# A layer of differential attention: FFN at other steps, a coefficient on GpSimd, and both maps' exponentials in SBUF

## The reference

```
q1,q2,k1,k2,v = xn @ Wqkv.T + b      # 16 q heads, 8 k heads of 128, 4 v heads of 256
p = softmax(q1 k1 / sqrt(128)) - lam * softmax(q2 k2 / sqrt(128))     # causal
o = rmsnorm(p @ v) * subln_w * (1 - lambda_init);  s = o @ out_w.T + out_b
g = silu(quant4(xn) @ quant4(Wffn).T + bias)   # blocks of 32 rounded to a 4-bit float
x = x + s * g
```

## Time and profile before

| | us |
|---|---|
| runs | 1752.3, 1755.01, 1758.83 |
| median | 1755.01 |
| the profiled execution's own time | 1754.4 |
| its span | 1752.6 |

### The profile page before, as it was taken

How to read it: one execution, slowest core, us unless ns; L and a number is a source line. 1 busy time by engine, 2 the same in 40 slices (tenths; PEclk the granted TensorE clock), 3 DMA queues, 4 the chain that set the end, 5 groups by cost and what they waited for, 6 DMA issues and landing times. The chain is left out here.

```text
span 1752.6 us, 28521 instructions
## 1 busy us (share of the span) xinstructions
PE 1538.7 (88%) x9137; PEld 899.8 (51%) x9153; DVE 1196.0 (68%) x3177; ACT 885.8 (51%) x2542; POOL 662.4 (38%) x1161
## 2 busy tenths in 40 slices
PE   2666588999989988999889988999989989899898
PEld 1343355555555555545555555545555546555554
DVE  4467777776777677776677667775777767675682
ACT  4563356535663456535664356634564356533561
POOL 2103542345324443344424443244424443243433
PEclk7778799999999999999999999999999999999999
DMA  7401334333342334333352334324342333422433
GB/s 250 140 4 27 64 67 82 61 88 70 50 91 55 84 73 82 64 78 72 55 87 57 84 73 79 68 46 100 55 85 54 95 63 65 80 54 67 64 76 73
DMA packets 385353, 130.63 MB, mean 75 GB/s; under 512 B 366354, under 2 KB 366900, under 8 KB 385204
## 3 DMA queue, kind: packets, MB, share of 16 engines
q1 hardware_dynamic: 385204, 128.81, 35.4%
HBM read 31.74 MB, written 8.39 MB: 23 GB/s over the span
## 5 line engine op out<-in xcount | busy, mean ns | idle before, releaser
L690 ACT ACTIVATE ph<-ps,small 128x128 f16<-128x128 f32 (+3 forms) x256 | 134.4, 525 | 395.0 <-DVE ps L981 394.4
L1168 POOL TENSOR_SCALAR norm<-psum_l,small 128x1 f32<-128x1 f32 x256 | 88.4, 345 | 584.9 <-ACT pp L681 584.9
L970 DVE CUSTOM_DVE_ANT_0 ps<-ps,mask,ssc 128x384 f32<-128x384 f32 (+3 forms) x512 | 279.7, 551 | 35.9 <-PE ps L547 35.4
L490 PE MATMUL ps<-xT,wqkv 128*128 128x512 f16 x768 | 297.6, 387 | 6.8 <-DVE qkv L940 6.4
L491 PE MATMUL ps<-xT,wqkv 128*128 128x512 f16 x768 | 296.4, 386 | 0.0
L492 PE MATMUL ps<-xT,wqkv 128*128 128x512 f16 x768 | 295.5, 385 | 0.0
L940 DVE SCALAR_TENSOR_TENSOR qkv<-ps,bsc,qkv 128x512 f16<-128x512 f32 x192 | 143.3, 750 | 187.0 <-ACT qkv L658 187.0
L490 PE MATMUL ps<-qkv,pT 128*128 128x256 f16 x640 | 179.6, 281 | 74.3 <-DMA pT<-ph 73.5
L545 PE MATMUL ps<-qkv 128*128 128x384 f16 (+3 forms) x512 | 155.2, 309 | 56.5 <-DVE ph L987 53.6
L490 PE MATMUL ps<-wout,heads 128*128 128x512 f16 x512 | 194.1, 379 | 0.5 <-DVE small L956 0.5
L491 PE MATMUL ps<-wout,heads 128*128 128x512 f16 x512 | 194.0, 379 | 0.0
(11 more groups left out here) (147 smaller groups left out, 3146.9 us busy)
## 6 DMA issues: line engine op xcount, KB each, us to landing
xin<-in_L_attn_hidden_states SPq DMA_DIRECT2D x8, 1024.0 KB, 5.8
xres<-in_L_attn_hidden_states SPq DMA_DIRECT2D x32, 256.0 KB, 2.8
out_x<-res SPq DMA_DIRECT2D x32, 256.0 KB, 2.4
qkv<-in_L_attn_Wqkv_w SPq DMA_DIRECT2D x8, 512.0 KB, 7.3
heads<-in_L_attn_Wqkv_w SPq DMA_DIRECT2D x8, 512.0 KB, 10.7
pT<-ph SPq DMA_TRANSPOSE x256, 2.7
heads<-on SPq DMA_TRANSPOSE x256, 2.5
qkv<-in_L_attn_out_w SPq DMA_DIRECT2D x4, 512.0 KB, 5.6
```

The costliest lines, as they stand in the source:

```text
L490: mm(out, ah, bh, start=start and j == 0, stop=False)
L690: run(ph[:, n % PH, 0:w], sc_ps[u][:, 1, 0:w], ACT.Copy, scale=sigma).then_inc(ph_hi, 1)
L970: nc.vector.tensor_tensor_reduce(sc, sc, mask[:, S - w:S], ssc[:, c:c + 1], BIG, ALU.add, ALU.min, ebias[:, u, m:m + 1]).then_inc(max_done, 1)
```

## The change

Six things are changed together.

- The ffn fills move from steps 10 to 13 to steps 22 to 25, and group 2's v fills from 15 and 16 to 14 and 15. In steps 24 and 25 the ffn fill is ahead of the next batch's k fill in the list. The transposes of `aq` move one step later, to 10 and 11.
- Reciprocal and coefficient are computed by GpSimd in `eps_of`, by a pow with exponent -1 and a tensor_scalar, ahead of the instruction that stood there alone.
- `pp` holds both maps. Map 0 is now first in `maxima` and `exps`. Both exponentials go to `pp`, combine reads and writes `pp`, and `p_hi` and `p_lo` read it.
- `scores(n)` waits for the exponentials of step n - 2.
- `xh` lies in `gate`, with a wait of the ffn fill's first write for the transpose of `x`; the first and second split move one step earlier. In the last batch the first load of `xres` waits for the second ffn fill.
- `square_o` writes its unused squares to PSUM, and the identity of the setup lies in `pT`.

```
-PH = 4 - AHEAD
+PH = 2
-FFN_STEP = 10
+FFN_STEP = 22
-        at = (None, PROJ_AT, PROJ_AT[:6] + (7, 8), (0, 1, 1, 2, 3, 3, 4, 5))[g]
+        at = (None, PROJ_AT, PROJ_AT, (0, 1, 1, 2, 3, 3, 4, 5))[g]
-X_SPLIT = {15: 0, 17: 1, 18: 2, 19: 3}
+X_SPLIT = {14: 0, 16: 1, 18: 2, 19: 3}
-        pp = sb("pp", [P, S], F32)
+        pp = sb("pp", [P, 2, S], F32)
-        xh = [t[:].bitcast(F16).rearrange("p (s h) -> p s h", s=2) for t in (res, xres)]
-        xh += [aq[:, 2 * u:2 * u + 2, :].bitcast(F16) for u in range(2)]
+        xh = [gate[:, k, :].bitcast(F16).rearrange("p (s h) -> p s h", s=2) for k in range(NT)]
+        junk = [ps[:, 6, E:2 * E], ps[:, 7, E:2 * E]]
...
-                if b == B - 1 and s == LAST_STEP:
+                if b == B - 1 and s == FFN_STEP + 3:
+                    sp.wait_ge(fill_done, fill_of("ffn", b, 0, 1) + 1)
                     residual(b, 0)
-                for k in {FFN_STEP - 1: (0, 1), FFN_STEP: (2, 3)}.get(s, ()):
+                for k in {10: (0, 1), 11: (2, 3)}.get(s, ()):
...
-                wait(pe, ph_lo, n - 1)
+                wait(pe, exp_done, 2 * n - 2)
...
-                for a, m in enumerate((1, 0)):
+                for a, m in enumerate((0, 1)):
                     act.wait_ge(max_done, 2 * n + a + 1)
                     sc = sc_ps[u][:, m, 0:w]
-                    if m == 0:
-                        wait(act, comb_done, n)
-                    run(sc if m else pp[:, 0:w], sc, ACT.Exp, bias=ebias[:, u, m:m + 1], scale=-1.0,
+                    wait(act, ph_lo if m else comb_done, n)
+                    run(pp[:, m, 0:w], sc, ACT.Exp, bias=ebias[:, u, m:m + 1], scale=-1.0,
...
-                run(ph[:, n % PH, 0:w], sc_ps[u][:, 1, 0:w], ACT.Copy, scale=sigma).then_inc(ph_hi, 1)
+                run(ph[:, n % PH, 0:w], pp[:, 1, 0:w], ACT.Copy, scale=sigma).then_inc(ph_hi, 1)
...
                     wait(dve, gated, f.gate - NT + 1)
+                    if f.gate // NT + 1 < B:
+                        dve.wait_ge(xT_done[j], 16 * (f.gate // NT + 2))
...
-                dve.wait_ge(exp_done, 2 * n + 2)
-                nc.vector.reciprocal(recip[:], l2).then_inc(recip_done, 1)
-                dve.wait_ge(recip_done, n + 1)
-                ts(coef[:, u:u + 1], l1, recip[:], neglam, ALU.mult, ALU.mult).then_inc(coef_done, 1)
                 dve.wait_ge(coef_done, n + 1)
-                stt(out=sc_ps[u][:, 1, 0:w], in0=sc_ps[u][:, 1, 0:w], scalar=coef[:, u:u + 1], in1=pp[:, 0:w],
+                stt(out=pp[:, 1, 0:w], in0=pp[:, 1, 0:w], scalar=coef[:, u:u + 1], in1=pp[:, 0, 0:w],
...
-                stt(out=ph[:, n % PH, w:2 * w], in0=sc_ps[u][:, 1, 0:w], scalar=sigma, in1=ph[:, n % PH, 0:w],
+                stt(out=ph[:, n % PH, w:2 * w], in0=pp[:, 1, 0:w], scalar=sigma, in1=ph[:, n % PH, 0:w],
...
                 pool.wait_ge(exp_done, 2 * n + 2)
+                pt(recip[:], l2, minusone, ALU.pow).then_inc(recip_done, 1)
+                pool.wait_ge(recip_done, n + 1)
+                nc.gpsimd.tensor_scalar(coef[:, n % 2:n % 2 + 1], recip[:], l1, neglam, ALU.mult, ALU.mult)\
+                  .then_inc(coef_done, 1)
                 wait(pool, on_lo, n - 5)
                 nc.gpsimd.tensor_scalar(nr[:, 0:1], l1, l1, eg[:, g:g + 1], ALU.mult, ALU.mult).then_inc(eps_done, 1)
```

More of the change, by code:

```diff
@@ L207, in build @@
         on = sb("on", [P, 2, 2, 2, P], F16)
-        junk = sb("junk", [P, E], BF16)
         v32 = sb("v32", [P, 2, E], F32)
@@ L211, in build @@
         xres = sb("xres", [P, HID], F32)
-        ident = sb("ident", [P, P], F32)
         mask = sb("mask", [P, S], BF16)
@@ L218, in build @@
         bnat = v32[0:34, 0, 0:P]
-        lam4, lam2 = pp, v32[:, 1, :]
+        lam4, lam2 = pp[:, 0, :], v32[:, 1, :]
         t2 = v32[:].rearrange("p a e -> p (a e)")
@@ L222, in build @@
                for t in (xres, res) for u in range(2)]
-        xh = [t[:].bitcast(F16).rearrange("p (s h) -> p s h", s=2) for t in (res, xres)]
-        xh += [aq[:, 2 * u:2 * u + 2, :].bitcast(F16) for u in range(2)]
+        xh = [gate[:, k, :].bitcast(F16).rearrange("p (s h) -> p s h", s=2) for k in range(NT)]
         spare = pT[:, 1, :, :].rearrange("p c t -> p (c t)").bitcast(F32)
         bT = spare[:, 0:34]
+        ident = spare[:, 256:384]
         babs, bgrp, bound = [spare[:, 64 + 32 * t:96 + 32 * t].rearrange("p (g c) -> p g c", g=G) for t in range(3)]
@@ L396, in _ @@
                 load_w(n)
+            for k in range(NT):
+                sp.wait_ge(xT_done[k], 16)
             sp.dma_start(gate[:], fw_d.rearrange("(k p) h -> p k h", p=P)).then_inc(ld_fw, 16)
@@ L452, in _ @@
                 if s == 0 and b:
-                    sp.wait_ge(xT_done[1], 16 * (b + 1))
                     residual(b - 1, 0)
@@ L588, in _ @@
                 for c in range(4):
-                    last = tr(setup_bank(m)[:, c * P:(c + 1) * P], slot(kind, n // 2)[:, n % 2, c * P:(c + 1) * P], ident[:])
+                    last = tr(setup_bank(m)[:, c * P:(c + 1) * P], slot(kind, n // 2)[:, n % 2, c * P:(c + 1) * P], ident)
                 last.then_inc(su_pe, 1)
@@ L689, in p_hi @@
                     act.wait_ge(pT_done[(n - PH) % AHEAD], 16 * ((n - PH) // AHEAD + 1))
-                run(ph[:, n % PH, 0:w], sc_ps[u][:, 1, 0:w], ACT.Copy, scale=sigma).then_inc(ph_hi, 1)
+                run(ph[:, n % PH, 0:w], pp[:, 1, 0:w], ACT.Copy, scale=sigma).then_inc(ph_hi, 1)
             def square_o(n):
                 act.wait_ge(pv_done, n + 1)
-                run(junk[:], o_ps[n % 2], ACT.Square, scale=SQ_SCALE, accum_out=sumsq[:, n % 2:n % 2 + 1])\
+                run(junk[n % 2], o_ps[n % 2], ACT.Square, scale=SQ_SCALE, accum_out=sumsq[:, n % 2:n % 2 + 1])\
                     .then_inc(sq_done, 1)
@@ L709, in x_hi @@
                     act.wait_ge(res_free, 16 + 16 * (n - NT))
-                    act.wait_ge(q_done, 2 * NT)
+                    act.wait_ge(wT_done, 16 * NT)
                 run(xh[n % NT][:, 0, :], xin[:, n % NT, :], ACT.Copy, scale=X_SCALE).then_inc(xh_hi, 1)
@@ L974, in combine @@
                 u, w = n % 2, place(n)[3]
-                l1, l2 = psum_l[:, n % 6, 0:1], psum_l[:, n % 6, 1:2]
-                dve.wait_ge(exp_done, 2 * n + 2)
-                nc.vector.reciprocal(recip[:], l2).then_inc(recip_done, 1)
-                dve.wait_ge(recip_done, n + 1)
-                ts(coef[:, u:u + 1], l1, recip[:], neglam, ALU.mult, ALU.mult).then_inc(coef_done, 1)
                 dve.wait_ge(coef_done, n + 1)
-                stt(out=sc_ps[u][:, 1, 0:w], in0=sc_ps[u][:, 1, 0:w], scalar=coef[:, u:u + 1], in1=pp[:, 0:w],
+                stt(out=pp[:, 1, 0:w], in0=pp[:, 1, 0:w], scalar=coef[:, u:u + 1], in1=pp[:, 0, 0:w],
                     op0=ALU.mult, op1=ALU.add).then_inc(comb_done, 1)
@@ L1019, in _ @@
                 elif kind == "scores":
+                    maxima(0, 0)
                     maxima(0, 1)
-                    maxima(0, 0)
                 elif kind == "ahead":
@@ L1024, in _ @@
                         combine(a - 1)
+                        maxima(a, 0)
+                        p_lo(a - 1)
                         maxima(a, 1)
-                        p_lo(a - 1)
-                        maxima(a, 0)
                 elif kind == "w":
@@ L1051, in _ @@
                 if n + AHEAD < NSTEPS and not late:
-                    maxima(n + AHEAD, 1)
+                    maxima(n + AHEAD, 0)
                 if n + AHEAD - 1 < NSTEPS:
@@ L1058, in _ @@
                     if late:
-                        maxima(n + AHEAD, 1)
-                    maxima(n + AHEAD, 0)
+                        maxima(n + AHEAD, 0)
+                    maxima(n + AHEAD, 1)
                 prepare(b, s, "maxima")
@@ L1077, in _ @@
             pt = nc.gpsimd.tensor_tensor
-            for m in (ident, mask):
-                nc.gpsimd.memset(m[:], 0.0).then_inc(consts, 1)
+            for m in (ident, mask[:]):
+                nc.gpsimd.memset(m, 0.0).then_inc(consts, 1)
             pool.wait_ge(consts, 2)
             for m in (ident,):
-                nc.gpsimd.affine_select(out=m[:], in_=m[:], compare_op=ALU.not_equal, fill=1.0, base=0,
+                nc.gpsimd.affine_select(out=m, in_=m, compare_op=ALU.not_equal, fill=1.0, base=0,
                                         pattern=[[-1, P]], channel_multiplier=1).then_inc(consts, 1)
@@ L1163, in eps_of @@
                 g = place(n)[1]
-                l1, nr = psum_l[:, n % 6, 0:1], norm[:, n % 6, :]
+                l1, l2, nr = psum_l[:, n % 6, 0:1], psum_l[:, n % 6, 1:2], norm[:, n % 6, :]
                 pool.wait_ge(exp_done, 2 * n + 2)
+                pt(recip[:], l2, minusone, ALU.pow).then_inc(recip_done, 1)
+                pool.wait_ge(recip_done, n + 1)
+                nc.gpsimd.tensor_scalar(coef[:, n % 2:n % 2 + 1], recip[:], l1, neglam, ALU.mult, ALU.mult)\
+                  .then_inc(coef_done, 1)
                 wait(pool, on_lo, n - 5)
```

## The result

The changed kernel takes 1789.07 us (median of 4 runs, 1788.16 to 1789.64) against 1755.44 us (the kernel before, four runs made beside it): ratio 1.0186, with a 95% interval of 1.0172 to 1.0199, 34 us slower. The forecast was 1750, no change; the time lies 4 us above the range, which ended at 1785.

What follows compares the result with a forecast made beforehand. TensorE was taken to bound the kernel, idle where the softmax relay is late. Middle batches -3 us, batch 0 -8 and the last +6.6 gave -4.4 from 1754.4: 1750 us, range 1712 to 1785.

Steps and rivals of the forecast that it cites:

- part 2: Both exponentials in SBUF: earlier scores gains 0, combine and p_lo on two SBUF operands lose 0.7 us per batch.
- the slower rival: Shared SBUF interface: combine, p_lo and GpSimd's work block each other, 4.5 us a batch, 1780 us; chance 0.24.
- the sum: Six middle batches -3 us, batch 0 -8, last batch +6.6: together -4.4 from 1754.4 us.
- The bound of 0.55 us lost per instruction: Most a combine or p_lo would lose, from one L1007 taking 1.23 us beside a wide v_low.
- Steps 10 to 16 would gain 8.8 us: Middle batch, FFN and one v fill moved out: 41.0 us become 32.2, with 2.1 us of waiting.
- Steps 22 to 31 would lose 8.3: Middle batch: FFN links make the relay late; 8.3 us lost, FFN's 3.4 us of work included.
- the wait for k1: TensorE's new wait at step 25 for VectorE's low half of the k fill: 4.6 us, once a batch.
- The last batch would lose 6.6: Relay alone on the path from step 22: 31.3 us against 16.4, 15.4 lost, 8.8 gained.
- TensorE's wait before step 14: Sign of the forecast: this wait falls from 3.4 to about 1 us.
- Batch 0: Gain of 8 us: steps 1 to 9 shrink 4.5, steps 10 to 16 shrink 11.5, less 8.3.
- the 0.3 us a step: Coefficient on GpSimd: gain counted per step with a q or k fill, where VectorE's fill hides its 1.2 us.
- The faster rival: Tanh does not hold the relay at steps 22 to 25: 1690 us, or 1715 if half the loss goes; chance 0.25.

Runs made afterwards that it cites:

- ffn_coef: The whole change, but map 1's exponential back in PSUM, with the old order of the maps and old wait of scores: 1756.96 us, ratio 1.0015.
- run 7: Not a follow-up run: the words say that, of the run's 32 first gating operations, 7 start within 0.1 us of a combine.
- scores_wait: The whole change, but scores waits for the low half of two steps before again: 1790.52 us, ratio 1.0191.
- ffn_exp: The whole change, but reciprocal and coefficient back on VectorE: 1784.53 us, ratio 1.0169.
- two_in_combine: The whole change, but combine writes PSUM, so only combine reads two SBUF operands, and scores waits for the low half: 1772.76 us, ratio 1.0109.
- two_in_lo: The whole change, but map 1's exponential in PSUM and combine writing SBUF, so only the low half reads two SBUF operands: 1766.26 us, ratio 1.0073.
- narrow_after: The whole change, but GpSimd's v_low and both gating operations on one column from batch 1 on, other columns left out: 1705.37 us, ratio 0.9723.
- narrow_ffn_coef: ffn_coef with GpSimd's v_low and both gating operations on one column from batch 1 on, other columns left out: 1701.92 us, ratio 0.9703.

## Why the prediction was wrong

**The step that failed** is in part 2: "I take 0.7 us lost per batch", for combine and `p_lo` on two SBUF operands. The runs give 3.9 us in a middle batch: against `ffn_coef` the whole change is longer by 0.5, 0.8, 0.4 and 2.2 us in the four stretches of the table, and by 32 us in all where the sum had 6. That is 26 of the 39 us between 1750 and 1789. The mechanism, its rows and its price stood there as the slower rival, with a chance of 0.24, and its price of the interface, 4.5 us a batch or 36 in all, is close to the 32 measured. Its 1780 is 9 us short because the rest of the sum was 13 us too low, told below.

Three things made the chosen term small.

- I thought that GpSimd is mostly waiting in the late stretches, so that few instructions meet. The rival's "a quarter of them hit, 0.5 us each" was nearly right: 103 of 512, a fifth, by 0.5 us each. They are not spread by chance: nearly the same steps are hit in every batch, since one step's exponentials release the coefficient, then combine on VectorE and gating or `finish` on GpSimd. They do not meet every time either: of the 32 first gating operations of the run 7 start within 0.1 us of a combine, as at 1126.58 and 1126.65.
- The bound of 0.55 us lost per instruction came from one row; the longest combine here loses 1.1 us.
- I priced only VectorE's side. GpSimd's L1174 takes 415 ns on average against 233 in `ffn_coef`, and all of GpSimd is busy 963.5 us against 881.6, 82 us more for the same work. L1174 is ahead of `normalised` and the next exponentials.

Where the extra time falls counts for more than how much it is. In a middle batch combine and `p_lo` lose 3.5 us in steps 0 to 9, which cost 0.5 us of time, and 1.5 us in steps 22 to 31, which cost 2.2, more than VectorE's own loss.

The range did not hold the rival either: its price, 4.5 us a batch, was in the text, but the range ended 5 us above its 1780.

**What held**, point by point, without part 2, as `ffn_coef` shows it:

- Steps 10 to 16 would gain 8.8 us in a middle batch; they gain 9.2.
- Steps 22 to 31 would lose 8.3 and lose 8.7. The working has the 0.7 of part 2 in one place only, the later start of these steps (the slower rival counts it as 6 in all), so without it they would lose 7.6, and the term was 1.1 too small. The links are those named: ScalarE idle before tanh, k's high half behind it and TensorE's bank behind that. That idle time was put at around 3 us and is 3.9; the wait for k1 was put at 4.6 and is 4.47 (4.26 in `ffn_coef`).
- The last batch would lose 6.6 and loses 6.3.
- The new instructions of GpSimd take 0.55 and 0.34 us, and from the start of pow to `eps_of` it is 0.97 us (1125.38 to 1126.35), set at 0.96.
- TensorE's wait before step 14 is 1.13 us, set at about 1.
- The wait of `scores` is gone and gave nothing (`scores_wait`).

**What was off beside it.** Without part 2 the sum is 10 us faster than before; `ffn_coef` is 2.7 us slower in its profiled run, so 13 us of the 39 are not the interface's. About 7 are the 1.1 us above, 2 are steps 17 to 21, 5 are batch 0, and steps 10 to 16 give 2 back. Batch 0 gains 2.9 us in `ffn_coef`, not 8: up to step 9 it gains 2.0 of 4.5, perhaps because VectorE's quantising waits for GpSimd's rounding in those steps (not tested), and steps 10 to 16 gain 10.2 of 11.5. The middle steps 17 to 21, taken as free, lose 0.4; the FFN move alone has 0.9 there. The coefficient without the FFN move is worth more in the late steps than the 0.3 us a step: 3.7 us in ten steps. Two counts of the working are slightly off and change nothing: steps 10 to 16 and 22 to 31 hold 34 combines and `p_lo`s, not 36, and GpSimd has 32 wide instructions in a batch, not 28.

**The Trainium skill's rule**, "SBUF — State Buffer", section "Who interferes with whom", was on the right side. In this case's traces one of the two waits for about the rest of the other, as it says: a combine of 0.61 us took 1.52 beside a wide gating operation of 1.04, 0.91 more. The section lets the one that starts first have the interface. Here VectorE was lengthened although its record begins 0.07 us before GpSimd's, so the recorded starts do not tell who holds it.

**The faster rival** was wrong as it stood: the tanh did hold the relay. It can be let go by a second buffer, and that `ffn_coef` then takes 1714 us where the rival said "if half, 1715" is luck, since the rival spoke of the change as it was.

## What to carry to other kernels

Before two operands of a VectorE instruction are put in SBUF, look at what GpSimd runs from the event that releases that instruction: if one event releases both, they meet at the same steps in every round, and the price is up to the length of GpSimd's instruction, where the path is late. Price GpSimd's side too. A buffer with one owner that GpSimd must give back (here `t2`) puts what stands in GpSimd's queue ahead of every instruction behind it on the other engine; a second buffer, or one step between two uses, took 2.4% off `ffn_coef` here. A change of several parts is best valued part by part in each stretch: the coefficient measured 0 in sum and was +3.2 and -3.7 us in two places of each batch.

The best version measured that does all the work is `two_tanh`: the change with map 1 left in PSUM and a second tanh buffer, 1714 us against 1754, ratio 0.9758 [0.9735, 0.9780].

## What the runs showed of the hardware that was not expected

- The two costs of the interface add to more than their sum: 16 us and 9 us one at a time, 32 together, and 40 where the FFN fills are spread and more instructions meet (141 against 103). I can say where it shows, in every stretch, but not by which chain; it stays open.
- A combine of 128 columns was never lengthened in the whole change (347 ns on average of 64, 0.35 us at most), where `p_lo` of 128 was, by over 0.1 us, in 28 of 64 (the two lines of 128 columns above). The first starts just behind the coefficient, when GpSimd still works on single columns; the second meets `norm` or a wide instruction. `ffn_exp` speaks for this: with the coefficient on VectorE, 13 of its 64 combines of 128 are lengthened, up to 1.14 us.
- One-column instructions of GpSimd are lengthened by VectorE too: L1174 takes 233 ns on average in `ffn_coef`, 367 in `two_in_combine`, 415 in the whole change, but 247 in `two_in_lo`, so most of it comes with combine's operands. In `narrow_after` it is 370, and that kernel is 3.5 us slower than `narrow_ffn_coef` (1705.4 against 1701.9), for this and all else.
- In step 25 TensorE idles 1.8 us before 1109.0, then 4.5 us from 1109.8 on. The granted clock goes to its low level at 1110.2, early in the second wait, and stays there until 1117.0, so the first matmuls of 512 columns after it take 0.61 us. In `two_tanh`, with a wait of 0.9 at that place, the window's granted clock is 1.00 throughout.
